# Laying a kernel's inputs out on the host: fewer, wider loads and no weight turns on TensorE

## The chip, the cores and the metric

The kernel runs on one core of a Trainium2 chip. The metric is the device time of one execution in microseconds, lower is better. A core has the engines TensorE (PE in the profile; PEld is its weight load), VectorE (DVE), ScalarE (ACT), GpSimd (POOL) and SyncE (SP). SP, ACT and POOL also issue DMAs; the suffix q in a row of the profile (SPq, ACTq) marks such an issue, and "landing" is the moment at which the whole transfer has arrived.

## The reference

Four layers in a row on x of 32 sequences x 32 tokens x 256 features (B, S, D). Each sequence has a role (1 or 2 of 3 possible) and a target code.

```python
# layers 0, 2 and 3: an adapter whose weights are picked by the role of the sequence
h = gelu(x @ W_down[role] + b_down[role])          # 256 -> 128, exact gelu
y = x + h @ W_up[role] + b_up[role]                # 128 -> 256
x = (y - mean(y)) * rsqrt(var(y) + 1e-5) * gamma[role] + beta[role]

# layer 1: attention over 32 tokens and two 4x-wide MLPs, the same weights for all
q, k, v = x @ Wq, x @ Wk, x @ Wv
a = softmax(q @ k.T / 16) @ v @ Wp + bp
cms = gelu(a @ cW1 + cb1) @ cW2 + cb2 + one_hot(code)
mod = gelu(concat(a, cms) @ mW1 + mb1) @ mW2 + mb2
x = clip(x + cms + mod, 0, 1)
```

## The kernel before

All tensors are float32; products whose precision matters are split into a high and a low part of a faster format (suffixes _h and _l in the names) and take three matmuls.

**Sorting by role.** The 1024 tokens are cut into 8 windows of 128 tokens (4 sequences). VectorE sorts the sequences by role at run time (`find_windows`, L1064 to L1109), so that six windows hold one role each and need one set of adapter weights, and two mixed windows (`MESSY`, 4 and 5) need two. One small TensorE product (`find_order`, L653) and one VectorE operation (L1114) turn the sort into token numbers `from_row_i`, by which POOL gathers the windows of x from HBM (L1485, tile `x_tok`). The roles of the windows go to SP, which reads them into registers and fetches each window's adapter weights (`fetch`, L559: one DMA for W_down, one for W_up).

**Set-up of layer 1.** Wq Wk^T and Wv Wp are multiplied once ("fold", L696), since the attention only needs the products. For this Wq, Wk and Wv are first turned on TensorE (`fold_transpose`, L684), copied out by ScalarE (L908), and then multiplied. The small vectors (biases, gamma, beta) are loaded as rows into `vec_rows`, 16 DMAs on three queues; one product picks the rows for each window (`chunk_vectors`, L670), and one turn makes `vecs`, one column for each vector of 128 (`vectors`, L646).

**Order.** Nothing is scheduled by a tool. The list in `plan` (L114) gives the steps in order, and each engine runs its part of each step in that order; `("fold", 0, 0)` is a step's name and its arguments. Engines meet on semaphores only. So a step of TensorE that waits holds up each step behind it in the list. The adapter chain of a window in layer 0 is `load` (turn x), `down`, gelu on ScalarE, `up`, statistics on VectorE (L1256), `center` (L1321), `turn`.

**DMA order.** SP issues its DMAs in the order of its block (L532), ACT those of L870 on, POOL five vector loads (L1481) and then the gathers.

Of the kernel before, what the change touches and what calls it, by code (L numbers as in the profile page):

```python
# [16 lines left out]
F32 = mybir.dt.float32  # L17
F32R = mybir.dt.float32r
I32 = mybir.dt.int32
# [5 lines left out]
P = 128  # L25
B, S, D = 32, 32, 256
N = B * S
R = 3
# [126 lines left out]
def build(nc, a, out):  # L155

    steps = plan()
    with ExitStack() as ctx:
# [20 lines left out]
        roles_i = place("roles_i", [P, B], I32)  # L179
# [23 lines left out]
        role_col_i = place("role_col_i", [B, 2], I32)  # L203
# [52 lines left out]
        wdA = [place(f"wdA{i}", [P, KD, P], F32) for i in range(WSLOTS)]  # L256
        wuA = [place(f"wuA{i}", [P, D], F32) for i in range(WSLOTS)]
        wdB = [place(f"wdB{i}", [P, KD, P], F32) for i in range(WSLOTS)]
        wuB = [place(f"wuB{i}", [P, D], F32) for i in range(WSLOTS)]
        last_at = {(layer, n): stage_at + 4 * D * (2 * len(LAST) * i + 2 * m) for i, layer in enumerate((2, 3))  # L260
                   for m, n in enumerate(range(SLOTTED, PASSES))}
        wd_last = {key: place(f"wd_last{key[0]}_{key[1]}", [P, KD, P], F32, offset) for key, offset in last_at.items()}
        wu_last = {key: place(f"wu_last{key[0]}_{key[1]}", [P, D], F32, offset + 4 * D) for key, offset in last_at.items()}
# [35 lines left out]
        vec_rows = place("vec_rows", [ROWS, P], F32, g_at)  # L299
# [7 lines left out]
        wT = {w: place(f"wT_{w}", [P, KD, D], F32) for w in "qkv"}  # L307
# [24 lines left out]
        codes_in = sem("codes_in")  # L332
        vectors_in = sem("vectors_in")
        mlp_vectors_in = sem("mlp_vectors_in")
# [3 lines left out]
        wdA_in = [sem(f"wdA_in{i}") for i in range(WSLOTS)]  # L338
        wuA_in = [sem(f"wuA_in{i}") for i in range(WSLOTS)]
        wdB_in = [sem(f"wdB_in{i}") for i in range(WSLOTS)]  # L340
        wuB_in = [sem(f"wuB_in{i}") for i in range(WSLOTS)]
        wd_last_in = {key: sem(f"wd_last_in{key[0]}_{key[1]}") for key in last_at}
        wu_last_in = {key: sem(f"wu_last_in{key[0]}_{key[1]}") for key in last_at}
        x_in = [sem(f"x_in{i}") for i in range(TSLOTS)]
        bu_in = sem("bu_in")
        bu_late_in = sem("bu_late_in")
# [13 lines left out]
        vectors_ps = sem("vectors_ps")  # L360
        vectors_ready = sem("vectors_ready")
        chunk_vecs_ready = sem("chunk_vecs_ready")
        wT_ps = sem("wT_ps")
        wT_ready = sem("wT_ready")
# [72 lines left out]
        def weights_of(layer, c):  # L437

            found = []
            for n in pass_of(layer, c):  # L440
                if (layer, n) in last_at:
                    found.append((wd_last[layer, n], wu_last[layer, n], wd_last_in[layer, n], wu_last_in[layer, n], 16))
                    continue
                kind, i = home(layer, n)
                down, up, down_in, up_in = (wdA, wuA, wdA_in, wuA_in) if kind == "A" else (wdB, wuB, wdB_in, wuB_in)
                s = i % WSLOTS
                found.append((down[s], up[s], down_in[s], up_in[s], 16 * (i // WSLOTS + 1)))
            return found
# [51 lines left out]
        def square(w):  # L500
            return tiled("qkvp".index(w) // 2)[:, KD * ("qkvp".index(w) % 2):KD * ("qkvp".index(w) % 2 + 1), :]
# [24 lines left out]
        down_w = {0: "L0_cond_W_down", 2: "L2_cond_W_down", 3: "L3_cond_W_down"}  # L526
        up_w = {0: "L0_cond_W_up", 2: "L2_cond_W_up", 3: "L3_cond_W_up"}

# [4 lines left out]
        def _(sp):  # L533
            sp.dma_start(roles_i[:, :], a["itok_B_1_2"].partition_broadcast(P)).then_inc(ids_in, 16)
            sp.dma_start(square("k"), a["L1_cond_Wk"].rearrange("(k p) n -> p k n", p=P)).then_inc(square_in["k"], 16)
            sp.dma_start(role_col_i[:, 1:2], a["itok_B_17_1546"].rearrange("(b o) -> b o", o=1)).then_inc(codes_in, 16)

            def piece(p):
                slot, _ = filling(p)
                src, view, _ = pieces[p]  # L540

                if p == 1:
                    sp.wait_ge(wT_ps, 2)
                elif p == 2:
                    sp.wait_ge(fold_ps, KD)
                elif p > 2:
                    sp.wait_ge(w_ready, p - STAGE + 1)
                sp.dma_start(view(slot), src).then_inc(stage_in[slot], 16)
# [10 lines left out]
            def fetch(layer, r, down, up, down_in, up_in):  # L559
                sp.dma_start(down[:, :, :],  # L560
                             a[down_w[layer]].rearrange("r (k p) n -> r p k n", p=P)[bass.ds(r, 1), :, :, :]
                             .rearrange("r p k n -> (r p) k n")).then_inc(down_in, 16)
                sp.dma_start(up[:, :],
                             a[up_w[layer]][bass.ds(r, 1), :, :].rearrange("r p n -> (r p) n")).then_inc(up_in, 16)

            def adapter_weights(layer, n):
# [3 lines left out]
                down, up, down_in, up_in = (wdA, wuA, wdA_in, wuA_in) if kind == "A" else (wdB, wuB, wdB_in, wuB_in)  # L570
# [6 lines left out]
                fetch(layer, role[column], down[slot], up[slot], down_in[slot], up_in[slot])  # L577
# [7 lines left out]
            for v, w in ((GAMMA2, "L2_cond_gamma"), (BETA2, "L2_cond_beta")):  # L585
                for m in range(KD):
                    sp.dma_start(vec_rows[R * (v + m):R * (v + m + 1), :],
                                 a[w][:, m * P:(m + 1) * P]).then_inc(vectors_in, 16)
# [19 lines left out]
            for layer, n in last_at:  # L608
                fetch(layer, role[passes_of(layer)[n][1]], wd_last[layer, n], wu_last[layer, n],
                      wd_last_in[layer, n], wu_last_in[layer, n])  # L610
# [13 lines left out]
        def _(pe):  # L624
# [21 lines left out]
            def vectors():  # L646
                pe.wait_ge(constants, 2)
                pe.wait_ge(vectors_in, (3 + 4 * KD) * 16)
                pe.wait_ge(mlp_vectors_in, 5 * 16)
                take(0, vectors_ready, 1)  # L650
                pe.transpose(bank[0][:, 0:ROWS], vec_rows[:, :], ident[0:ROWS, 0:ROWS]).then_inc(vectors_ps, 1)

            def find_order():  # L653
                pe.wait_ge(sorts_ready, 1)
                take(1, rows_in_ready, 1)
                pe.matmul(bank[1][:, 0:FULL], seat[:, :], rows_of[:, :], start=True, stop=True).then_inc(order_ps, 1)
# [9 lines left out]
            def chunk_vectors():  # L666
                pe.wait_ge(role_hot_ready, 1)
                pe.wait_ge(vectors_in, (3 + 4 * KD) * 16)
# [898 lines left out]
```

## Time and profile before

| | us |
|---|---|
| device time, median of 3 runs | 197.14 (196.89 to 197.19) |
| span of the profiled execution, first to last instruction | 196.6 |
| PE busy | 184.1 (94%) |
| DVE busy | 114.4 (58%) |
| ACT busy | 80.7 (41%) |
| POOL busy | 44.2 (22%) |

The profile holds no other time of the profiled execution than its span of 196.6 us; the median lies 0.54 us above it. Times in rows count from the first instruction. In rows of windows, counts of instructions stand in brackets, and the last three numbers are PE's granted clock, the DMA engines' busy share and GB/s. Busy PE is not PE at its peak: ends of matmuls are modelled. A float32 matmul is two PE instructions.

### The profile page before, as it was taken

Reading aid. Unit: us, or ns where it says so; the run is one execution under the profiler, and the core shown is the slowest. Engines: PE = TensorE matmul, PEld = TensorE weight load, DVE = VectorE, ACT = ScalarE, POOL = GpSimd, SP = SyncE. Lnnn points to the kernel's source line nnn. Section 1 sums busy time; section 2 is a strip of 40 time slices with the busy share of each in tenths; the row PEclk is TensorE's granted clock in tenths of the full one; section 3 lists DMA queues with packets and bytes.
Section 4 is the critical chain, followed back from the end, with each engine's and each line's share of the span. In section 5 each row is a group of like instructions: output and inputs, shape, how many; then the busy total and the mean of one; then the engine's idle time right before and its main releaser. Section 6 shows DMA issues by size and latency. Waiting matters only on the chain.

```text
span 196.6 us, 3109 instructions
## 1 busy us (share of the span) xinstructions
PE 184.1 (94%) x1031; PEld 157.7 (80%) x1031; DVE 114.4 (58%) x283; ACT 80.7 (41%) x164; POOL 44.2 (22%) x74
## 2 busy tenths in 40 slices
PE   7877999989999999999999999999999999999960
PEld 7755878878988888778888888888888989999840
DVE  2994998989648807983193522041442146569972
ACT  0733656544698405672045543003546242222420
POOL 8472848200000006000140000000110012234552
PEclk9999999999999999999999999999999999999995
DMA  3687389996300230330000060000100005433002
GB/s 110 224 243 242 97 259 294 245 312 187 107 3 8 100 107 0 107 110 0 0 0 3 0 196 18 0 0 3 55 0 0 3 0 141 125 85 107 28 27 80
DMA packets 18585, 17.82 MB, mean 91 GB/s; under 512 B 2049, under 2 KB 16970, under 8 KB 18570
## 3 DMA queue, kind: packets, MB, share of 16 engines
q1 hardware_dynamic: 16720, 14.60, 24.3%
q0 software_dynamic: 1024, 2.37, 4.5%
q10 hardware_dynamic: 826, 0.67, 1.1%
q8 instruction: 8, 0.13, 0.3%
q14 instruction: 7, 0.06, 0.1%
HBM read 16.58 MB, written 1.05 MB: 90 GB/s over the span
## 4 chain that ended last, share of the span: by engine, by line
PE 79%; DVE 8%; DMA 5%; issue 3%; ACT 2%; POOL 1%; ACTq 0%; DVEq 0%; POOLq 0%
PE bank L636 20%; PE bank L638 19%; PE bank L637 19%; PE bank L748 5%; PE bank L764 5%; DMA stage<-in_L_cond_Wq 2%; PE bank L741 2%; PE bank L815 2%; PE bank L804 2%; DMA x_tok<-in_x,from_row_i 2%; PE bank L774 1%; DVE yA L1321 1%; PE bank L743 1%; DMA out<-yB,from_row_i 1%; DVE cms_l L1423 1%
## 5 line engine op out<-in xcount | busy, mean ns | idle before, releaser
L1402 DVE TENSOR_TENSOR g_l<-g_full,g_h 128x512 fp32r<-128x512 f32 x32 | 21.8, 690 | 36.1 <-ACT g_h L1028 36.0
L1025 ACT ACTIVATE g_full<-bank,vecs 128x512 f32<-128x512 f32 x32 | 22.1, 691 | 43.5 <-PE bank L638 39.9
L1514 POOL TENSOR_TENSOR mvA<-mvA,power 128x1 f32<-128x1 f32 x16 | 9.4, 589 | 72.0 <-DVE mvA L1257 72.0
L1028 ACT ACTIVATE g_h<-bank,vecs 128x512 fp32r<-128x512 f32 x32 | 22.0, 686 | 0.0
L1541 POOL TENSOR_TENSOR x1T<-x1T,cms_full 128x512 f32<-128x512 f32 x4 | 6.0, 1497 | 57.4 <-DVE cms_full L1417 57.3
L636 PE MATMUL bank<-g_h,mw_h 128*128 128x256 f32 (+1 forms) x48 | 16.0, 334 | 0.0
L638 PE MATMUL bank<-g_h,mw_l 128*128 128x256 f32 (+1 forms) x48 | 15.3, 318 | 0.0
L637 PE MATMUL bank<-g_l,mw_h 128*128 128x256 f32 (+1 forms) x48 | 15.3, 318 | 0.0
L636 PE MATMUL bank<-ao_h,mw_h 128*128 128x512 f32 x32 | 13.1, 411 | 0.0
L636 PE MATMUL bank<-ao_h,cw_h 128*128 128x512 f32 x32 | 12.8, 400 | 0.1
L638 PE MATMUL bank<-ao_h,mw_l 128*128 128x512 f32 x32 | 12.5, 391 | 0.0
L637 PE MATMUL bank<-ao_l,mw_h 128*128 128x512 f32 x32 | 12.5, 390 | 0.0
L638 PE MATMUL bank<-cms_h,mw_l 128*128 128x512 f32 x32 | 12.5, 390 | 0.0
L638 PE MATMUL bank<-ao_h,cw_l 128*128 128x512 f32 x32 | 12.5, 390 | 0.0
L636 PE MATMUL bank<-cms_h,mw_h 128*128 128x512 f32 x32 | 12.5, 390 | 0.0
L637 PE MATMUL bank<-ao_l,cw_h 128*128 128x512 f32 x32 | 12.5, 390 | 0.0
L636 PE MATMUL bank<-g_h,cw_h 128*128 128x512 f32 x32 | 12.5, 389 | 0.0
L638 PE MATMUL bank<-g_h,cw_l 128*128 128x512 f32 x32 | 12.5, 389 | 0.0
L637 PE MATMUL bank<-cms_l,mw_h 128*128 128x512 f32 x32 | 12.5, 389 | 0.0
L637 PE MATMUL bank<-g_l,cw_h 128*128 128x512 f32 x32 | 12.4, 389 | 0.0
L1321 DVE TENSOR_SCALAR yA<-bank,mvA 128x256 f32<-128x256 f32 x16 | 8.6, 540 | 3.1 <-POOL mvA L1514 2.8
L1417 DVE TENSOR_TENSOR cms_full<-bank,target 128x512 f32<-128x512 f32 x4 | 2.8, 692 | 12.9 <-PE bank L638 12.9
(265 smaller groups left out, 442.8 us busy)
## 6 DMA issues: line engine op xcount, KB each, us to landing
stage<-in_L_cond_mW SPq DMA_DIRECT2D x6, 512.0 KB
stage<-in_L_cond_cW SPq DMA_DIRECT2D x4, 512.0 KB
wdA<-in_L_cond_W_down SPq DMA_DIRECT2D x14, 128.0 KB
wuA<-in_L_cond_W_up SPq DMA_DIRECT2D x14, 128.0 KB
wdB<-in_L_cond_W_down SPq DMA_DIRECT2D x12, 128.0 KB, 2.5
wuB<-in_L_cond_W_up SPq DMA_DIRECT2D x12, 128.0 KB, 2.8
wd_last<-in_L_cond_W_down SPq DMA_DIRECT2D x4, 128.0 KB, 2.3
wu_last<-in_L_cond_W_up SPq DMA_DIRECT2D x4, 128.0 KB, 2.5
```

Of the source, the lines that this page charges most:

```text
L636: pe.matmul(dst, w[0], x[0], start=first, stop=False)
L637: pe.matmul(dst, w[0], x[1], start=False, stop=False)
L638: return pe.matmul(dst, w[1], x[0], start=False, stop=last)
L741: pe.matmul(bank[b][:, m * P:(m + 1) * P], x[:, m, :], ident[:, :], start=(m == 0), stop=False, is_transpose=True, skip_group_check=True)
L748: mm = pe.matmul(bank[b][:, D + part * P:D + (part + 1) * P], wd[:, k, :], x[:, k, :], start=False, stop=(k == KD - 1), skip_group_check=True)
L764: mm = pe.matmul(dst, h[:, part, :], wu[:, :], start=False, stop=(part == len(turns) - 1), skip_group_check=True)
L1025: act.activation(g_full[n % 2][:, 0:width], bank[b][:, 0:width], ACT.Gelu, bias=bias)
L1028: act.activation(g[0][:, j, 0:width], bank[b][:, 0:width], ACT.Gelu, bias=bias).then_inc(g_high, 1)
L1321: dve.tensor_scalar(yA[k][:, :], bank[chain_bank(layer, c)][:, 0:D], mvA[:, k, 0:1], mvA[:, k, 2:3], ALU.subtract, ALU.mult).then_inc(norm ...
L1402: dve.tensor_tensor(g[1][:, j, 0:width], g_full[n % 2][:, 0:width], g[0][:, j, 0:width].bitcast(F32), ALU.subtract).then_inc(g_ready, 1)
L1514: pool.tensor_tensor(mv[:, k, 2:3], mv[:, k, 1:2], power[:, :], ALU.pow).then_inc(done, 1)
L1541: pool.tensor_tensor(half, half, cms_full[:, m, :], ALU.add).then_inc(sum_ready, 1)
```

## The change

The host, which before passed every input as it was, now passes repacked copies of the same numbers:

- `ids`: 128 rows of 34 numbers, the 32 roles and then this row's role and code. One DMA on SP in place of three on SP and ACT.
- `squares`: Wq, Wk and Wv already turned, Wp as it is, each as 128 rows of 2 KB. Four DMAs remain, first or second on their queues (before, 256 rows of 1 KB each, with Wv fourth and Wp fifth or later). The turns on TensorE and their copies on ScalarE go; the tiles `wT` are loaded directly, with one for p, and no longer share the `stage` slots.
- `vec_rows` and `vecs`: the rows that the picking products need in one DMA, and the turned vectors in another, both on ACT. The turn of `vec_rows` on TensorE and its copy on ScalarE go, with POOL's five loads.
- `b_up`: one DMA in place of three.
- `adapters`: a role's W_down and W_up side by side, 128 rows of 2 KB. `fetch` issues one DMA in place of two, with one semaphore. The 30 fetches of the program were 60 DMAs and are 30.

In `plan`, the two steps `fold_transpose` 0 and 1 and the three warm-up products go, and both steps of `fold` 0 stand ahead of `order`.

```diff
-        ("warm", 10), ("fold_transpose", 0), ("fold_transpose", 1), ("warm", 3), ("order",), ("pick_vecs",),
-        ("fold_transpose", 2), ("spread",), ("fold", 0, 0), ("first_hot",), ("fold", 0, 1), ("fold_low", 0),
-        ("fold", 1, 0), ("chunk_vecs",), ("vectors",), ("sort_rest",), ("load", 0, 0), ("fold", 1, 1),
+        ("warm", 10), ("fold", 0, 0), ("fold", 0, 1), ("order",), ("pick_vecs",), ("spread",), ("first_hot",),
+        ("fold_low", 0), ("fold", 1, 0), ("chunk_vecs",), ("sort_rest",), ("fold", 1, 1), ("load", 0, 0),
...
-            sp.dma_start(roles_i[:, :], a["itok_B_1_2"].partition_broadcast(P)).then_inc(ids_in, 16)
-            sp.dma_start(square("k"), a["L1_cond_Wk"].rearrange("(k p) n -> p k n", p=P)).then_inc(square_in["k"], 16)
-            sp.dma_start(role_col_i[:, 1:2], a["itok_B_17_1546"].rearrange("(b o) -> b o", o=1)).then_inc(codes_in, 16)
+            sp.dma_start(ids[:, :], a["ids"]).then_inc(ids_in, 16)
+            sp.dma_start(wT["k"][:, :, :], square_from("k")).then_inc(square_in["k"], 16)
+            sp.dma_start(wT["p"][:, :, :], square_from("p")).then_inc(square_in["p"], 16)
...
-            def fetch(layer, r, down, up, down_in, up_in):
-                sp.dma_start(down[:, :, :],
-                             a[down_w[layer]].rearrange("r (k p) n -> r p k n", p=P)[bass.ds(r, 1), :, :, :]
-                             .rearrange("r p k n -> (r p) k n")).then_inc(down_in, 16)
-                sp.dma_start(up[:, :],
-                             a[up_w[layer]][bass.ds(r, 1), :, :].rearrange("r p n -> (r p) n")).then_inc(up_in, 16)
+            def fetch(layer, r, w, w_in):
+                sp.dma_start(w[:, :], a["adapters"][(0, 2, 3).index(layer)][bass.ds(r, 1), :, :]
+                             .rearrange("r p n -> (r p) n")).then_inc(w_in, 16)
...
-            for m, w in enumerate(("L0_cond_b_up", "L2_cond_b_up", "L3_cond_b_up")):
-                sp.dma_start(bu_rows[0:2 * R, m, :],
-                             a[w].unsqueeze(0).to_broadcast([2, R, D])).then_inc(bu_late_in if m else bu_in, 16)
-            sp.dma_start(square("p"), a["L1_cond_Wp"].rearrange("(k p) n -> p k n", p=P)).then_inc(square_in["p"], 16)
+            sp.dma_start(bu_rows[0:2 * R, :, :], a["b_up"]).then_inc(bu_in, 16)
             piece(0)
...
-                    pe.wait_ge(wT_ready, 2 + n)
-                    if n:
-                        pe.wait_ge(square_in["p"], 16)
+                    pe.wait_ge(square_in[left], 16)
+                    pe.wait_ge(square_in[right], 16)
...
-            act.dma_start(role_col_i[:, 0:1], a["itok_B_1_2"].rearrange("(b o) -> b o", o=1)).then_inc(ids_in, 16)
-            act.dma_start(square("q"), a["L1_cond_Wq"].rearrange("(k p) n -> p k n", p=P)).then_inc(square_in["q"], 16)
...
+            for w in "qv":
+                act.dma_start(wT[w][:, :, :], square_from(w)).then_inc(square_in[w], 16)
+            act.dma_start(vec_rows[:, :], a["vec_rows"][0:PER_ROLE * R, :]).then_inc(vectors_in, 16)
+            act.dma_start(vecs[:, :], a["vecs"]).then_inc(vecs_in, 16)
...
-                dve.wait_ge(ids_in, 32)
+                dve.wait_ge(ids_in, 16)
```

TensorE's queue at the start of the program, before. `stage_121` holds Wq and Wk, `stage_122` Wv; the product with `rows_of` is the step `order`.

```order
L644 MATMUL bank<-warm 128x128 x9
L692 MATMUL bank<-ident,stage_121 128x128 [waits square_in_q,constants]
L692 MATMUL bank<-ident,stage_121 128x128 x3
L692 MATMUL bank<-ident,stage_121 128x128 [waits square_in_k,constants]
L692 MATMUL bank<-ident,stage_121 128x128 x3
L644 MATMUL bank<-warm 128x128 [waits warm_ready]
L644 MATMUL bank<-warm 128x128 x2
L656 MATMUL bank<-rows_of,seat 128x6 [waits sorts_ready]
L692 MATMUL bank<-ident,stage_122 128x128 [waits square_in_v,constants]
L692 MATMUL bank<-ident,stage_122 128x128 x3
L706 MATMUL bank<-wT_k,wT_q 128x256 [waits wT_ready,rows_in_ready]
L706 MATMUL bank<-wT_k,wT_q 128x256 x3
```

The same place in the changed kernel. `x_tok_189` and `x_tok_190` are the first two gathered windows of x.

```order
L613 MATMUL bank<-warm 128x128 x9
L654 MATMUL bank<-wT_k,wT_q 128x256 [waits square_in_k,square_in_q]
L654 MATMUL bank<-wT_k,wT_q 128x256 x3
L618 MATMUL bank<-rows_of,seat 128x6 [waits sorts_ready]
L654 MATMUL bank<-wT_p,wT_v 128x256 [waits square_in_p,square_in_v]
L654 MATMUL bank<-wT_p,wT_v 128x256
L632 MATMUL bank<-role_pick,vec_rows 128x66 [waits vectors_in,role_hot_ready]
L654 MATMUL bank<-wT_p,wT_v 128x256 x2
L669 MATMUL bank<-ident,x_tok_189 128x128 [waits x_in0,constants,rows_in_ready]
L669 MATMUL bank<-ident,x_tok_189 128x128
L669 MATMUL bank<-ident,x_tok_190 128x128 [waits x_in1,xA_ready]
L669 MATMUL bank<-ident,x_tok_190 128x128
```

The product of `order` now has four matmuls of 256 columns ahead of it, where it had eight turns and three warm-ups, and between the two loads of x no fold matmul is left: all eight stand ahead of the first load.

SP's queue from the moment at which the windows' roles are known, before:

```order
L554 TENSOR_LOAD chunk_role_i [waits chunks_ready]
L560 ISA
L560 DMA wdA_124<-in_L_cond_W_down 128x2x128
L563 DMA wuA_128<-in_L_cond_W_up 128x256
L560 ISA
L560 DMA wdA_125<-in_L_cond_W_down 128x2x128
L563 DMA wuA_129<-in_L_cond_W_up 128x256
```

And changed:

```order
L534 TENSOR_LOAD chunk_role_i [waits chunks_ready]
L540 ISA
L540 DMA wA_123<-in_adapters 128x512
L540 ISA
L540 DMA wA_124<-in_adapters 128x512
```

Each pair of DMAs of a window has become one DMA of the same bytes.

## Rows read from the trace of the kernel before

**Rows 1.** Windows: stretch, length, busy us of PE, PEld, DVE, ACT, POOL, clock, DMA.
```profile
14.00:17.00 3.00, 2.02 (x16) 1.81 (x17) 1.73 (x10) 0.53 (x2) 1.75 (x2) 1.00 1.01 326
...
20.00:25.00 5.00, 4.82 (x35) 3.96 (x34) 4.83 (x18) 3.46 (x11) 3.59 (x5) 1.00 0.47 121
...
80.00:180.00 100.00, 99.85 (x534) 85.54 (x533) 45.03 (x86) 35.64 (x66) 10.99 (x14) 1.00 0.15 44
```
**Rows 2.** Timeline, 0 to 20 us: start, us, engine, line, what, count, idle before.
```profile
0.73 0.42 SPq L534 DMA_DIRECT2D roles_i<-in_itok_B  x1
...
1.06 4.21 PE L644 MATMUL bank<-warm 128*128 128x128 f32 x20 [1.06 <-DVE warm L1065]
...
1.20 0.47 ACTq L874 DMA_DIRECT2D stage<-in_L_cond_Wq  x1
1.21 0.42 SPq L535 DMA_DIRECT2D stage<-in_L_cond_Wk  x1
...
4.48 0.18 DVE L1076 TENSOR_SCALAR roles<-roles_i 128x32 f32<-128x32 int32 x1 [1.88 <-DMA role_col_i<-in_itok_B]
...
6.93 0.83 PE L644 MATMUL bank<-warm 128*128 128x128 f32 x6
...
7.13 0.28 DVE L1103 TENSOR_SCALAR rows_of<-window_of,is_full,row_col 32x6 f32<-32x6 f32 x1
...
7.70 0.38 PE L656 MATMUL bank<-rows_of,seat 32*128 32x6 f32 x2
...
8.62 1.06 POOL L1485 DMA_INDIRECT x_tok<-in_x,from_row_i  x1 [2.61 <-DVE from_row_i L1114]
...
14.29 0.01 SPq L560 DMA_DIRECT2D wdB<-in_L_cond_W_down  x1
...
15.71 0.01 SPq L563 DMA_DIRECT2D wuB<-in_L_cond_W_up  x1
15.75 0.37 ACT L923 COPY xA<-bank 128x256 f32<-128x256 f32 x1 [1.59 <-PE bank L719]
...
17.31 0.62 ACT L940 ACTIVATE hA<-bank,chunk_vecs 128x128 f32<-128x128 f32 x2 [1.19 <-PE bank L748]
...
18.47 0.43 DVE L1256 BATCH_NORM_STATS2 statsA<-bank 128x6 f32<-128x256 f32 x1 [2.68 <-PE bank L764]
```
**Rows 3.** DMA issues: what, queue, count, KB each, median us to landing.
```profile
wdB<-in_L_cond_W_down SPq DMA_DIRECT2D x12, 128.0 KB, 2.5
...
stage<-in_L_cond_Wq ACTq DMA_DIRECT2D x1, 256.0 KB, 4.7
stage<-in_L_cond_Wk SPq DMA_DIRECT2D x1, 256.0 KB, 4.4
...
x_tok<-in_x,from_row_i POOLq DMA_INDIRECT x8, 3.9
...
roles_i<-in_itok_B SPq DMA_DIRECT2D x1, 16.0 KB, 2.9
role_col_i<-in_itok_B ACTq DMA_DIRECT2D x1, 0.1 KB, 3.7
```
**Rows 4.** The chain of waits: start, us, what.
```profile
8.62 3.50 DMA x_tok<-in_x,from_row_i
...
12.67 0.87 PE bank L706 x4
```
**Rows 5.** Timeline near the end of the program.
```profile
179.29 0.37 SPq L560 DMA_DIRECT2D wdB<-in_L_cond_W_down  x1
...
183.39 1.06 PE L748 MATMUL bank<-zB,wdB 128*128 128x128 f32 x8
```
**Rows 6.** Windows again, around the last matmuls.
```profile
189.00:191.00 2.00, 1.30 (x8) 0.70 (x6) 1.38 (x5) 0.37 (x1) 1.36 (x3) 1.00 0.18 66
191.00:192.40 1.40, 0.00 (x0) 0.00 (x0) 1.15 (x4) 0.00 (x0) 1.17 (x1) 1.00 0.00 0
192.40:194.00 1.60, 0.00 (x0) 0.00 (x0) 0.82 (x2) 0.00 (x0) 0.58 (x1) 0.50 0.57 164
```

More of the change, by code:

```diff
@@ L178, in build @@
         scratch = at[0]
-        roles_i = place("roles_i", [P, B], I32)
+        ids = place("ids", [P, B + 2], I32)
+        roles_i = ids[:, 0:B]
+        role_col_i = ids[0:B, B:B + 2]
         roles = place("roles", [P, B], F32)
@@ L306, in build @@
         y_T = place("y_T", [P, KD, HALF], F32, at[0])
-        wT = {w: place(f"wT_{w}", [P, KD, D], F32) for w in "qkv"}
+        wT = {w: place(f"wT_{w}", [P, KD, D], F32) for w in "qkvp"}
         wqk = [place(f"wqk_{x}", [P, KD, D], F32R) for x in "hl"]
@@ L569, in adapter_weights @@
                 slot = i % WSLOTS
-                down, up, down_in, up_in = (wdA, wuA, wdA_in, wuA_in) if kind == "A" else (wdB, wuB, wdB_in, wuB_in)
+                w, w_in = (wA, wA_in) if kind == "A" else (wB, wB_in)
                 if i >= WSLOTS:
@@ L644, in keep_warm @@
                     pe.matmul(bank[7][:, 0:P], warm[:, :], warm[:, :], start=True, stop=True)
[L646 to L651, printed above, removed]
             def find_order():
                 pe.wait_ge(sorts_ready, 1)
-                take(1, rows_in_ready, 1)
-                pe.matmul(bank[1][:, 0:FULL], seat[:, :], rows_of[:, :], start=True, stop=True).then_inc(order_ps, 1)
+                take(2, rows_in_ready, 1)
+                pe.matmul(bank[2][:, 0:FULL], seat[:, :], rows_of[:, :], start=True, stop=True).then_inc(order_ps, 1)
             def rest():
@@ L761, in up @@
                 turns = weights_of(layer, c)
-                for part, (_, wu, _, w_in, filled) in enumerate(turns):
-                    pe.wait_ge(w_in, filled)
-                    mm = pe.matmul(dst, h[:, part, :], wu[:, :], start=False, stop=(part == len(turns) - 1),
+                for part, (w, _, _) in enumerate(turns):
+                    mm = pe.matmul(dst, h[:, part, :], w[:, D:2 * D], start=False, stop=(part == len(turns) - 1),
                                    skip_group_check=True)
@@ L859, in outer @@
                             mm.then_inc(outer_ps, 1)
-            do = {"warm": keep_warm, "vectors": vectors, "order": find_order, "rest": rest, "chunk_vecs": chunk_vectors, "seq_vecs": seq_vectors,
-                  "codes": codes_sorted, "fold_transpose": fold_transpose, "fold": fold,
+            do = {"warm": keep_warm, "order": find_order, "rest": rest, "chunk_vecs": chunk_vectors, "seq_vecs": seq_vectors,
+                  "codes": codes_sorted, "fold": fold,
                   "load": load, "down": down, "up": up, "turn": turn, "values": values, "project": project, "scores": scores, "mix": mix,
@@ L1557 @@
     arrays, aps = {}, {}
-    for name, value in inputs.items():
-        if name == "_lenS":
-            continue
+    laid = {name: np.asarray(value) for name, value in inputs.items()}
+    by_role = [(f"L{n}_cond_b_down", 1) for n in (0, 2, 3)]
+    for n in (0, 2):
+        by_role += [(f"L{n}_cond_gamma", KD), (f"L{n}_cond_beta", KD)]
+    vec_rows = [laid[name][:, m * P:(m + 1) * P] for name, tiles in by_role for m in range(tiles)]
+    vec_rows += [laid[f"L1_cond_{name}"].reshape(-1, P) for name in ("bp", "cb1", "cb2", "mb1", "mb2")]
+    vec_rows = np.concatenate(vec_rows)
+    ids = np.stack([laid["itok_B_1_2"], laid["itok_B_17_1546"]], axis=1)
+    packed = {
+        "x": laid["x"],
+        "ids": np.concatenate([np.broadcast_to(laid["itok_B_1_2"], (P, B)), np.tile(ids, (P // B, 1))], axis=1),
+        "vec_rows": vec_rows,
+        "vecs": vec_rows.T,
+        "b_up": np.stack([np.tile(laid[f"L{n}_cond_b_up"], (2, 1)) for n in (0, 2, 3)], axis=1),
+        "squares": np.stack([w.reshape(KD, P, D).transpose(1, 0, 2) for w in (
+            laid["L1_cond_Wq"].T, laid["L1_cond_Wk"].T, laid["L1_cond_Wv"].T, laid["L1_cond_Wp"])]),
+        "adapters": np.stack([np.concatenate([
+            laid[f"L{n}_cond_W_down"].reshape(R, KD, P, P).transpose(0, 2, 1, 3).reshape(R, P, KD * P),
+            laid[f"L{n}_cond_W_up"]], axis=2) for n in (0, 2, 3)]),
+    }
+    packed.update((name, laid[name]) for name in (
+        "L1_cond_cW1", "L1_cond_cW2", "L1_cond_mW1", "L1_cond_mW2", "L3_cond_ln_w", "L3_cond_ln_b"))
+    for name, value in packed.items():
         v = np.ascontiguousarray(value)
```

111 lines of the change are left out of this document (31 added, 80 removed).

## The prediction

> **What bounds the kernel now.** I read three things in this order. First the windows: from 80 to 180 us PE is busy 99.85 of 100 us [rows 1], so that stretch has no hole that an earlier load could fill, and its length is set by matmuls that the change does not touch. Then the chain of waits and the timeline of the first 20 us [rows 2], since the chain leaves PE there: it goes from the squares' DMAs to PE, from PE to VectorE's token numbers, to the first gather of x, and from there through the first windows of layer 0. VectorE's first statistics start at 18.47 after 2.68 us of idling for PE; from then on VectorE is the full engine (4.83 of 5 us from 20 to 25 [rows 1]) until the dense stretch of PE begins. So the front is one chain up to 18.47: what moves that start moves the rest of the program with it, one for one, and what does not move it is worth nothing. Last the tail, because the adapter fetches change there too.
>
> The sum is made against the span of 196.6 us, and 0.54 us is added to get to the median of 197.14.
>
> **The ids.** The sort waits for two DMAs. `roles_i`, issued at 0.73, lands 2.9 us later [rows 2, 3], at 3.63. The column of 32 single numbers lands 3.7 us after its own issue on ACT, and it is this one that VectorE waits for: `roles` starts at 4.48, with the column named as the releaser [rows 2]. The one DMA `ids` has `roles_i`'s place, its 128 rows and nearly its bytes, so I take its 2.9: the sort starts near 3.67, 0.8 us earlier. Bounds: 2.9 (gain 0.8) and the column's 3.7 (gain 0). `rows_of`, the sort's last result for the gathers, ends at 7.41 = 7.13 + 0.28 [rows 2]; it would end at 6.6.
>
> **PE ahead of `order`.** Today the product starts at 7.70, 0.3 us after `rows_of`, because the three warm-ups (six instructions, 6.93 to 7.76) stand ahead of it [rows 2]. In the changed kernel fold 0 stands there. The ten first warm-ups run from 1.06 to 5.27 [rows 2] and stay. Two fold matmuls (four instructions) take 0.87 us of the chain [rows 4], so fold's four take 1.74. It needs q and k, which now land at 1.20 + 4.7 = 5.90 and 1.21 + 4.4 = 5.61 [rows 2, 3]. q moves to the head of ACT's queue, 0.46 us earlier, with half the packets; k keeps its place. I take both at 5.3, hence fold from 5.3 to 7.05 and `order` at 7.1, against 7.70: gain 0.6. What the sort has won beyond that (ready at 6.6) is lost behind fold. Bounds: with q and k in before 5.27 the gain is 0.65; with them where they are now (5.90), fold ends at 7.65 and it is 0; a later landing is rival 3.
>
> **The gather and layer 0.** The first gather follows `order` by 0.92 us (8.62 against 7.70 [rows 2]) and its x lands after 3.50, at 12.12 [rows 4]. So it is issued at 8.0, and x lands at 11.5. POOL's five vector loads are worth nothing: POOL idles 2.61 us for VectorE's token numbers behind them [rows 2], and still will. The windows' weights move earlier as well, since the sort's roles do, and SP then issues one DMA for a window where it issued two; this is beside the path. Two things could pull at the gain. More adapter bytes are queued by the time the gathers' packets run: the median gather takes 3.9 [rows 3], and if the first goes from its 3.5 to 3.9, 0.4 is lost. And `fold` 1 no longer stands between the two loads of x: 0.87 us of PE [rows 4] that lay in the wait for the second gather, worth 0. I keep 0.6.
>
> **The rest at nothing.** The turns and copies of squares and vectors on PE and ACT: the cover is the gather's flight of 3.5 us, and the only turns on the path are those ahead of `order`, already counted. The loads of `b_up` and of the vectors' rows: no wait in the first 20 us is put down to one of them. The fetches for layers 2 and 3 land long before use. The closest is the last: issued at 179.29, its W_down lands after 2.5 us and is used in the second half of the eight instructions from 183.39 [rows 3, 5], about 183.9. The joined DMA carries 128 KB more, 0.4 us at the 326 GB/s of rows 1; even with 0.9 it is in by 182.7, 1.2 us early. If that cover went, the end would be later by the rest.
>
> **Sum.** 196.6 - 0.6 = 196.0 us of span, and 196.5 us of time.
>
> **The clock rule.** Rows first: the twenty first warm-up instructions take 4.21 us, 0.21 each, the six later ones 0.83, 0.14 each [rows 2]: the early ones run at the lower of the two levels (1.2 GHz), the later at 2.4. At the end the granted clock falls from 1.00 to 0.50 at 192.4, behind 1.30 us of busy PE from 189 to 191 and 1.4 us of none [rows 6]. The Trainium skill (TensorE: Matmul & The Clock Gate, Part 1: The HAM clock gate) says that the low level is the default and that activity alone lifts it. That speaks against the change, which takes filler out of the wait for x; by it the saving can turn into a loss (rival 2). By the three stretches of rows 1, where the clock is 1.00 even at two thirds of busy time, nothing would be lost.
>
> **Rival 1: SP's and ACT's stalls go too.** At 14.29 and 15.71 SP's DMA issues take 0.01 us, where they otherwise take 0.42, and come 1.4 us apart; in the same stretch ACT copies the second window only at 15.75, after 1.59 us of idling for a turn on PE, and the gelu starts at 17.31 after 1.19 [rows 2], while the DMA engines are full (1.01 of the time [rows 1]). If both come of SP's queue being full, half the DMAs end it, and the window chain gains at most the two waits, 2.8 us, and at least nothing. For: SP and ACT go on in the same moment (15.71, 15.75). Against: nothing names the cause, and the bytes stay the same. I take 1.2 more than the forecast: 195.3.
>
> **Rival 2: the clock falls while PE waits for x (slower).** Place: behind the last fold matmul. From 5.3 the folds (3.5 us), `order` (0.4 [rows 2]) and the chunk vectors' product (about as much) end near 9.6, at most 10. x lands at 11.5, and the second window near 13 (8.0, 1.06 for the first issue, 3.9). PE has some 3 us with the two turns of the first window in them and nothing else. The tail shows a fall behind 3.4 us that held 1.3 [rows 6]. Against it: the wait for the first x today, behind folds and small products, costs no clock. Price: PE is busy 2.02 us from 14 to 17 [rows 1], and at half the clock that is 2.0 us more at most, and 0 where it hides behind the gathers; I take 1.5. It decides from a loss of 0.6 on. Time: 197.1 - 0.6 + 1.5 = 198.0.
>
> **Rival 3: fold holds up `order`.** All four squares are now asked for at once, with cW1 behind them. Today's landings of q and k have v beside them; one more square of 256 KB ahead of them is 0.8 us at 326 GB/s. Then k lands at 6.4, fold ends at 8.15, and the gather is 0.45 late: 197.6. If q and k come first on their two queues, as they are issued, they land between 5.3 and 5.9, and at the late end nothing changes: 197.1. The Trainium skill (DMA: Bandwidth & Descriptors, Issuing engines are not separate DMA queues) says that DMAs of different issuers interleave on the same engines. By it v competes with k and p with v, which leads to this rival; k's 4.4 [rows 3] agrees, as far as it goes, since q has the same bytes and 4.7.
>
> **Chances.** Forecast 47%, with its own range 196.2 to 196.9. Rival 1 20%. Rival 2 14%. Rival 3 19%, of which 13 end near no change and 6 slower. A measurement of this kernel can tell about 0.2% (0.4 us) from no change. Faster than 196.75: 40 of the forecast's 47 and rival 1, 60%. Within 0.2%: 7 and 13, 20%. Slower than 197.53: 14 and 6, 20%. The range runs from 195.2 to 197.9: it leaves out the lower part of rival 1 and the upper of rival 2, under 2 in 10.
>
> **What would show each step.** `roles` starting near 3.7 and `rows_of` ending near 6.6: the ids. Fold's first matmul at 5.3 and `order` right behind its last, near 7.1: the hand-over; an `order` product later than 7.7 is rival 3. The gather at 8.0, the first statistics near 17.9, with VectorE idle ahead of them as now: the shift. Statistics near 16.7, with SP's issues evenly spaced: rival 1. A granted clock under 1.00 between 10 and 20 us: rival 2. If the statistics come 0.6 earlier and the end does not, the front is not one chain, and "one for one" is the wrong step; the place to look is then between 20 us and the dense stretch. The forecast is wrong altogether if the time moves while the first statistics stay.

## The result and the profile after

The changed kernel takes 199.98 us (median of 4 executions, 198.38 to 200.43) against 197.16 of the kernel before: 1.0111 times as long, 95% interval 1.0060 to 1.0161. Twelve more executions gave 199.99 and 1.0115 (1.0076 to 1.0153). The forecast was 196.5, with a range up to 197.9. The profiled execution has a span of 198.4 and a time of 200.24. In all later runs time and span differ by 1.8, of the kernel before too (109 executions beside the experiments: median span 195.3, median time 197.09). A ratio leaves out executions far above the fastest of its kernel; where the clock falls in most executions but not in all, these are ordinary ones, and there the median tells more.

The chain of waits of the changed kernel, 0 to 20 us, its pieces in order of time (start us, us, what):

```profile
1.05 4.63 PE bank L613 x20
5.68 2.13 PE bank L654 x8
7.82 0.33 PE bank L618 x2
...
8.69 1.15 POOL x_tok L1419
...
10.14 5.63 DMA x_tok<-in_x,from_row_i
...
15.91 0.66 PE bank L669 x2
...
17.21 0.85 PE bank L699 x4
```

The chain goes over the second gather, which takes 5.63 us. In the rows of before it went over the first (3.50 [rows 4]) and then over PE's work; in a second profile of that kernel (below) it goes over the second gather too, which takes 3.92 us there. The timeline of the same stretch (start us, us, engine, line, what; idle before it, ended by what):

```profile
3.45 0.18 DVE L1014 TENSOR_SCALAR roles<-ids 128x32 f32<-128x32 int32 x1 [0.86 <-DMA ids<-in_ids]
...
5.48 2.34 PE L654 MATMUL bank<-wT_k,wT_q 128*128 128x256 f32 x8
...
6.11 0.28 DVE L1041 TENSOR_SCALAR rows_of<-window_of,is_full,row_col 32x6 f32<-32x6 f32 x1
...
7.75 0.38 PE L618 MATMUL bank<-rows_of,seat 32*128 32x6 f32 x2
...
8.14 1.92 SPq L540 DMA_DIRECT2D wA<-in_adapters  x4
...
8.69 1.15 POOL L1419 DMA_INDIRECT x_tok<-in_x,from_row_i  x1 [5.42 <-DVE from_row_i L1052]
...
13.15 0.62 PE L669 MATMUL bank<-ident,x_tok 128*128 128x128 f32 x2 [2.21 <-DMA x_tok<-in_x,from_row_i]
...
15.91 0.66 PE L669 MATMUL bank<-ident,x_tok 128*128 128x128 f32 x2 [2.14 <-DMA x_tok<-in_x,from_row_i]
...
20.54 0.43 DVE L1193 BATCH_NORM_STATS2 statsA<-bank 128x6 f32<-128x256 f32 x1 [4.86 <-PE bank L714]
```

Against [rows 2]: the sort starts 1.03 us earlier and ends 1.02 earlier, but `order` is at 7.75 (7.70 before), since fold 0 is ahead of it until 7.82. The statistics come at 20.54, 2.07 later than in the row of before, and 3.8 later than in its second profile (16.71). The windows of the stretch (length, busy us of PE, PEld, DVE, ACT, POOL, then the granted clock, DMA share, GB/s) show what happens to PE while it waits:

```profile
10.00:12.00 2.00, 0.94 (x4) 0.49 (x3) 1.86 (x9) 0.72 (x2) 1.55 (x2) 1.00 0.93 319
12.00:14.00 2.00, 0.62 (x2) 0.25 (x2) 1.86 (x14) 0.19 (x1) 1.39 (x3) 0.80 1.05 398
14.00:16.00 2.00, 0.09 (x1) 0.12 (x2) 1.64 (x8) 0.18 (x1) 1.70 (x2) 0.50 0.91 305
16.00:18.00 2.00, 2.00 (x10) 2.00 (x11) 0.00 (x0) 0.37 (x1) 0.17 (x1) 0.50 0.37 105
18.00:20.00 2.00, 2.00 (x11) 2.00 (x10) 0.00 (x0) 0.74 (x2) 0.00 (x0) 0.50 0.00 0
20.00:25.00 5.00, 5.00 (x35) 4.25 (x34) 4.14 (x18) 2.42 (x7) 2.95 (x4) 1.00 0.09 24
```

With 0.94, 0.62 and 0.09 us of work in three times 2 us, the clock falls to 0.50 (1.2 GHz) and stays there until 20 us, over the first windows' products. Four of them on L699 take 0.85 us of the chain, where four take 0.44 from 27.84 on, at full clock. The DMA issues answer to [rows 3] (KB each, median us to landing; x before 3.9, q 4.7, k 4.4):

```profile
wA<-in_adapters SPq DMA_DIRECT2D x14, 256.0 KB, 4.0
...
wT_q<-in_squares ACTq DMA_DIRECT2D x1, 256.0 KB, 3.0
...
wT_k<-in_squares SPq DMA_DIRECT2D x1, 256.0 KB, 3.6
...
x_tok<-in_x,from_row_i POOLq DMA_INDIRECT x8, 4.4
```

### The profile page after: what moved, and what is told of

It is laid out like the page before. It is cut to its first block, busy times and chain, and to the rows that moved or that the text cites. A ratio compares the mean times of both kernels' runs of the same rounds, so it can differ in the third digit from the quotient of the medians.

```text
span 198.4 us, 2982 instructions
## 1 busy us (share of the span) xinstructions
PE 184.8 (93%) x1012; PEld 158.2 (80%) x1012; DVE 114.4 (58%) x283; ACT 79.4 (40%) x160; POOL 41.5 (21%) x69
## 4 chain that ended last, share of the span: by engine, by line
PE 81%; DVE 8%; DMA 4%; issue 2%; POOL 2%; ACT 1%; DVEq 0%; POOLq 0%; ACTq 0%
PE bank L605 20%; PE bank L607 19%; PE bank L606 19%; PE bank L699 6%; PE bank L714 5%; DMA x_tok<-in_x,from_row_i 3%; PE bank L613 2%; PE bank L692 2%; PE bank L765 2%; PE bank L754 2%; PE bank L724 1%; DVE yA L1258 1%; PE bank L694 1%; PE bank L654 1%; DMA out<-yB,from_row_i 1%
## 5 line engine op out<-in xcount | busy, mean ns | idle before, releaser
L1193 DVE BATCH_NORM_STATS2 statsA<-bank 128x6 f32<-128x256 f32 x16 | 6.8, 422 | 6.8 <-PE bank L714 6.5
```

The source lines that it names most:

```text
L1193: link(dve.bn_stats(st[:, k, 0:6], y))
```

## The experiments

The theories: G, the adapter fetches, which now leave SP at one of 256 KB per 0.52 us (8.14 to 10.24 for four), slow the gathers of x; C, the clock's fall in the wait is what costs; F, fold 0 ahead of `order` eats what the ids gain. "Gathers" below are the times from POOL's issue of the first and of the second gather to their turn on PE. Each ratio is to the kernel before on the same chip.

**Fillers (C).** The diff is in `plan`:

```diff
-("fold", 1, 1), ("load", 0, 0), ("load", 0, 1),
+("fold", 1, 1), ("warm", 8), ("load", 0, 0), ("warm", 6), ("load", 0, 1),
```

> The changed kernel with filler products on PE in its two waits for x: eight (16 instructions) behind the last fold matmul and six (12) between the turns of the first and of the second window. If the clock's fall is what costs (theory C), the granted clock stays 1.00 from 7 to 20 us, the products of the first windows take 0.45 again where they took 0.85, the first statistics come at 19.2 or before instead of 20.54, and the time falls by 1.3 or more, to 198.6. If the late landing of x is what costs (theory G: the second window's x at 15.8), the clock stays up too but PE still turns the second window at 15.9, and at most half of it comes back: statistics near 19.9, time near 199.4.

Measured: 197.86 us, ratio 1.0048 (1.0026 to 1.0071), clock 0.992 to 0.997 in all ten executions. Gathers 4.60 and 5.40 us, statistics at 18.50. The windows in which the clock had fallen, and two lines of the timeline:

```profile
12.00:14.00 2.00, 1.44 (x13) 1.28 (x13) 1.86 (x14) 0.00 (x0) 1.60 (x2) 1.00 1.02 367
14.00:16.00 2.00, 1.49 (x14) 1.31 (x12) 1.87 (x10) 0.37 (x1) 1.49 (x2) 1.00 0.83 308
```

```profile
15.81 0.41 PE L669 MATMUL bank<-ident,x_tok 128*128 128x128 f32 x2 [0.51 <-DMA x_tok<-in_x,from_row_i]
...
18.50 0.43 DVE L1193 BATCH_NORM_STATS2 statsA<-bank 128x6 f32<-128x256 f32 x1 [2.56 <-PE bank L714]
```

The second turn is where it was (15.81 against 15.91), and the statistics come 2.0 us earlier. So 2.1 us of the loss hang on the clock, more than the 1.3 of theory C, and the gathers are about as slow as without the fillers.

**Order first (F).** Three filler products are added ahead of it.

```diff
-("warm", 10), ("fold", 0, 0), ("fold", 0, 1), ("order",),
+("warm", 13), ("order",), ("fold", 0, 0), ("fold", 0, 1),
```

> The changed kernel with the order product ahead of fold 0 and three more filler products ahead of it. If fold 0 in front of it (at the low clock level until 6.4 us) is what ate the ids' gain (theory F), order runs at 6.7 instead of 7.75, the first gather goes at 7.6 instead of 8.69, and all that follows comes 1.0 earlier: first statistics at 19.5, time 199.0. If the landing of x is set by what the DMA engines carry (theory G), the adapters' fetches of SP are not earlier in this kernel (chunk_role_i has the same time), the gathers go ahead of them, and x comes earlier by more than 1.0: statistics near 18.7, time near 198.2. If neither, 200.

Measured: 198.10 us, 1.0037 (0.9996 to 1.0077). Its timeline:

```profile
6.34 0.38 PE L618 MATMUL bank<-rows_of,seat 32*128 32x6 f32 x2 [0.79 <-DVE rows_of L1041]
...
7.31 1.14 POOL L1419 DMA_INDIRECT x_tok<-in_x,from_row_i  x1 [4.05 <-DVE from_row_i L1052]
...
14.41 0.66 PE L669 MATMUL bank<-ident,x_tok 128*128 128x128 f32 x2 [2.60 <-DMA x_tok<-in_x,from_row_i]
```

The product now waits for `rows_of` and not for PE's queue, and the gathers start 1.4 us earlier. The second still takes 5.65 us, and the clock still falls in most executions: 194.5 us of span in the one at clock 0.995, 197.1 in one at 0.974. F holds: the edit alone repairs 1.9 us. Not all of it need be `order` itself, since the clock is at 0.981 or more in eight of ten executions, where it is in two of sixteen of the changed kernel.

**Fetches held (G).** In SP's loop over layer 0's fetches:

```diff
+                if n == 2:
+                    sp.wait_ge(x_in[1], 16)
                 adapter_weights(0, n)
```

> The changed kernel in which SP holds back the adapter fetches from the third window's on until the second window's x is in. Theory G: the six fetches of 256 KB that are issued from 8.1 to 11.1 us slow the gathers; with two of them only, x lands 3.5 to 4.0 us after its issue (first 12.4, second 14.1 instead of 15.8), the statistics come near 18.6 and the time is near 198.0 if nothing later waits for the held fetches. Theory C or F alone: the gathers land as before (13.1 and 15.8), time 200.

Measured: 195.22 us, 0.9903 (0.9869 to 0.9937): 4.8 us less than the changed kernel, and faster than the kernel before. I had expected 198.0. Its timeline:

```profile
12.32 0.41 PE L671 MATMUL bank<-ident,x_tok 128*128 128x128 f32 x2 [1.12 <-DMA x_tok<-in_x,from_row_i]
...
13.32 0.41 PE L671 MATMUL bank<-ident,x_tok 128*128 128x128 f32 x2 [0.59 <-DMA x_tok<-in_x,from_row_i]
...
16.17 0.43 DVE L1195 BATCH_NORM_STATS2 statsA<-bank 128x6 f32<-128x256 f32 x1 [0.25 <-PE bank L716]
```

Gathers of 3.37 and 2.92 us, though `order` is at 8.01 here. With x in time PE has work, and the clock held in four of five executions. The second turn comes 2.6 us earlier than in the changed kernel, which with the 2.1 us of the clock is about the 4.8. The hold thus mends two of the three causes.

**Rate or size of the pieces?** Four kernels change only how SP sends the adapters of layer 0. Two DMAs of 1 KB pieces for a role:

```diff
-                sp.dma_start(w[:, :], a["adapters"][(0, 2, 3).index(layer)][bass.ds(r, 1), :, :]
-                             .rearrange("r p n -> (r p) n")).then_inc(w_in, 16)
+                for lo in (0, D):
+                    sp.dma_start(w[:, lo:lo + D], a["adapters"][(0, 2, 3).index(layer)][bass.ds(r, 1), :, lo:lo + D]
+                                 .rearrange("r p n -> (r p) n")).then_inc(w_in, 16)
```

> The changed kernel with each role's adapters fetched by two DMAs of 1 KB pieces instead of one of 2 KB: same bytes, same layout in memory, twice the DMAs. If the joining of the fetches (quicker issue, 2 KB pieces) is what slows the gathers, the second window's x lands 3.9 to 4.4 after its issue (14.2) instead of 5.6, the first statistics come near 19, time near 198.5. If the squares' and the other loads' new times do it, or the clock alone, it stays at 200.

Two DMAs of 64 partitions, pieces of 2 KB (`lo in (0, P // 2)`, `w[lo:lo + P // 2, :]`):

> The changed kernel with each role's adapters fetched by two DMAs of 64 partitions with pieces of 2 KB, against the two DMAs of 128 partitions with pieces of 1 KB of an earlier run (x landed 3.3 and 4.0 us after issue, time 198.3): the same bytes at the same rate of issue, only the pieces differ. If the size of the pieces is what slows the gathers (G-size), they take 4.4 and over 5 us and the time is 199.7. If it is the rate at which bytes are queued (G-rate), they take 3.3 and 4.0 and the time is 198.3.

One or two DMAs of 8 bytes behind each fetch:

```diff
                 adapter_weights(0, n)
+                sp.dma_start(pace[0:1, 2 * n:2 * n + 2], a["ids"][0:1, 0:2]).then_inc(pace_in, 16)
```

> The changed kernel with its 2 KB pieces and one DMA for a role's adapters, but a DMA of 8 bytes behind each of the ten fetches of layer 0 on SP, which holds SP for about 0.4 us: a fetch every 0.9 us instead of every 0.5. If it is the rate at which SP queues bytes (256 KB in 0.5 us) that slows the gathers (theory G-rate), x lands as with two DMAs to a role: first 3.3 and second 3.9 after issue; time like that kernel's, 198.3, or less where the clock holds. If it is the size of the pieces (G-size), the gathers stay at 4.4 and 5.7 us and the time at 200.

> The changed kernel with joined 2 KB pieces in one DMA, and two DMAs of 8 bytes behind each of layer 0's fetches, so one fetch every 1.25 us (205 GB/s) where one small DMA gave 0.87 us (301 GB/s; x landed 3.75 and 4.85 us after issue, 199.7). Theory G-rate: at this rate the engines have room and x lands 3.4 and 3.9 us after issue; time 198.3 or less, since nothing but the clock and fold 0 is then left. If it is the joining itself that slows the gathers and not the rate, 4.4 or more for the second and 199.7 again.

| fetches | us per 256 KB | GB/s asked for | gathers, us | time, us | ratio |
|---|---|---|---|---|---|
| changed kernel | 0.52 | 500 | 4.46, 5.77 | 199.98 | 1.0111 |
| one small DMA between | 0.88 | 298 | 3.78, 4.90 | 199.70 | 1.0126 (1.0066 to 1.0186) |
| kernel before, second profile | 1.08 | 243 | 3.17, 4.05 | 197.13 | |
| two of 1 KB pieces | 1.04 | 252 | 3.27, 3.99 | 198.33 | 1.0015 (0.9970 to 1.0059) |
| two small DMAs between | 1.18 | 222 | 3.52, 3.83 | 198.44 | 0.9965 (0.9903 to 1.0028) |
| two of 64 partitions | 1.33 | 196 | 3.63, 3.90 | 198.62 | 1.0068 (1.0026 to 1.0109) |

The second gather goes with the rate and not with the pieces: 2 KB pieces at 196 and 222 GB/s let it land as quickly as 1 KB pieces do. Nor is it, at the full rate, the number of fetches already out: with order first the second gather was issued 0.7 us behind the first fetch (8.76 and 8.04) and took 5.65, with 1 KB pieces 1.5 us behind it (9.44 and 7.92) and took 3.99. My expectation that 0.88 us would be slow enough was wrong. From the two paced kernels, the timelines (second gather's issue, second turn; first the one of 0.88, then the one of 1.18):

```profile
10.13 0.97 POOL L1423 DMA_INDIRECT x_tok<-in_x,from_row_i  x1 [0.30 <-issue]
...
15.03 0.66 PE L673 MATMUL bank<-ident,x_tok 128*128 128x128 f32 x2 [2.15 <-DMA x_tok<-in_x,from_row_i]
```

```profile
9.56 0.97 POOL L1424 DMA_INDIRECT x_tok<-in_x,from_row_i  x1 [0.30 <-issue]
...
13.39 0.41 PE L674 MATMUL bank<-ident,x_tok 128*128 128x128 f32 x2 [1.35 <-DMA x_tok<-in_x,from_row_i]
```

The three slower rates do not bring the kernel back to 195, because the clock falls in most of their executions: with two small DMAs between, one at clock 0.997 took 195.19 us, nine at 0.973 to 0.982 took 197.21 to 199.54.

**The kernel before, again.**

> The kernel before, unchanged, for a second profile. The other executions of it have spans of 194.8 to 196.1, the profiled one that the prediction was worked out from 196.6. If that one had a rare wait in it (SP's and ACT's stall near 15.7 us), this profile shows the second window's copy on ACT near 14.5 instead of 15.75, the first statistics near 17.2 instead of 18.47, and a span of 195.2. If not, the statistics come at 18.4 again and the difference lies elsewhere.

Measured: 197.13 us, profiled span 194.8. Its timeline:

```profile
9.94 1.02 POOL L1485 DMA_INDIRECT x_tok<-in_x,from_row_i  x1 [0.30 <-issue]
...
13.99 0.41 PE L719 MATMUL bank<-ident,x_tok 128*128 128x128 f32 x2 [0.98 <-DMA x_tok<-in_x,from_row_i]
14.10 0.42 SPq L563 DMA_DIRECT2D wuB<-in_L_cond_W_up  x1
...
14.44 0.37 ACT L923 COPY xA<-bank 128x256 f32<-128x256 f32 x1 [0.81 <-PE bank L719]
...
16.71 0.43 DVE L1256 BATCH_NORM_STATS2 statsA<-bank 128x6 f32<-128x256 f32 x1 [0.95 <-PE bank L764]
```

The stall of SP and ACT in [rows 2] is not in it. So the rows of before come from an execution with a wait that not every execution of the kernel has. How rare it is is not shown: two executions have a profile, and 16 of the 109 others took over 198.2 us.

**Parts alone, on the kernel before.** The ids in one DMA:

> The kernel before with the ids alone in one DMA. rows_of is ready at 6.4 instead of 7.4, but the order product stands behind two turns of squares, that wait for q until 6.0, and six filler instructions: theory F (PE's queue ahead of order decides, not the ids) says order at 7.3 to 7.65 and a time within 0.4 of before, 196.7 to 197.0. If the ids alone were worth what they come earlier, order would be at 6.7 and the time 196.1.

Measured: 196.16 us, 0.9959 (0.9931 to 0.9988); `order` at 6.66. I had expected next to nothing. `rows_of` was ready at 6.07, and PE's turns and six fillers were through at about 6.7, so the queue held `order` back by 0.6 and not by more. The joined adapters (one DMA of 2 KB pieces in `fetch`):

> The kernel before with the adapters alone joined: one DMA of 2 KB pieces for a role in place of two of 1 KB, on all fetches, nothing else changed. Theory G says that this part alone makes the kernel slower: x lands 4.4 and over 5 us after issue instead of 3.2 and 4.0, the second window's turn is at 15.3 instead of 14.0, and the time is 198.4, up to 200 where the clock falls in the wait. If joining is harmless and the squares' earlier loads or the shorter PE work are the cause, it stays at 197.

Measured: 198.84 us, 1.0083 (1.0046 to 1.0120). Its second gather:

```profile
10.41 1.02 POOL L1489 DMA_INDIRECT x_tok<-in_x,from_row_i  x1 [0.30 <-issue]
...
16.22 0.41 PE L723 MATMUL bank<-ident,x_tok 128*128 128x128 f32 x2 [1.90 <-DMA x_tok<-in_x,from_row_i]
```

5.81 us: this part alone, in an otherwise unchanged kernel, makes the whole delay of the gather. It costs 1.4 us of time (197.41 for the kernel before on this chip) without a fall of the clock: the granted clock is 1.00 in every window of this profile from 0 to 22 us. The hold without the change:

> The kernel before with the adapter fetches held from the third window's on until the second window's x is in; nothing of the change. In the second profile of the kernel before x lands 3.2 and 4.0 us after issue. Theory G: the second falls to 3.0, its turn goes from 13.99 to 12.96 and the time from 197.0 to 196.1, so the changed kernel with the same hold (195.2) keeps 0.9 us that are the change's own (earlier ids, fewer issues). If the hold alone were the whole gain, this kernel would take 195.2 too.

Measured: 196.83 us, 0.9991 (0.9974 to 1.0008): nothing that counts, where I had expected 196.1. At 243 GB/s there is little to hold back. Ids, joined adapters and hold together:

> The kernel before with the ids in one DMA, the joined adapters and the hold of the fetches until the second window's x is in; squares, vectors and b_up as before. It tells what the rest of the change (squares turned on the host, fewer vector loads) is worth: if nothing, this kernel equals the changed one with order first and the hold, 194.7. If the rest is worth its PE work ahead of the first turns, it stands at 195.5 to 196.0.

Measured: 195.60 us, 0.9898 (0.9844 to 0.9951), within the 195.5 to 196.0 that was expected if the rest has a worth of its own.

**Together.** Order first and hold; the same with four and two fillers; order first, with each of the third to the sixth fetch held for its own gather (`if 2 <= n < len(EARLY): sp.wait_ge(x_in[n - 1], 16)`):

> The changed kernel with both repairs: the order product ahead of fold 0, and the adapter fetches from the third window's on held until the second window's x is in. If the two add up, the gathers go at 7.3 and x lands at 10.6 and 11.6, but PE is then in the folds until 10.7; the first statistics come at 14.7 to 15.2 instead of 16.2 and the time is 193.8. If the fetches' hold is then the limit (a later window's weights come late), 195.2, as with the hold alone.

> As the kernel before in this list, with four filler products behind the last fold matmul and two between the first two turns. If the clock falls there in some executions (theory C), they end that: time 193.8 with a narrower spread and clock 0.997. If it doesn't fall, the six fillers (0.28 us each) delay the turns by up to 1.0 us and it is slower than without: 194.5.

> The changed kernel with the order product ahead of fold 0, and each adapter fetch from the third to the sixth held until the x of the window before it is in (so one fetch of 256 KB per 1.27 us, the distance of the gathers, about 206 GB/s), in place of one hold of all of them that is followed by a burst. If the burst behind the single hold costs something (there the fourth window's turn of x waited at 17.57), this is the fastest kernel: 194.0 or less, against 194.7. If the single hold already takes all there is, 194.7.

Measured: 194.69 us, 0.9879 (0.9819 to 0.9940), statistics at 14.95, clock 0.991 to 0.994; 194.91 with fillers; 194.92 with the finer hold. The three can't be told apart, and none reached the best that was expected of it (193.8, 193.8 and 194.0). Against the 195.60 of the kernel with ids, joined adapters and hold alone, 0.9 us are left for the turned squares, the vectors and the place of `order`, though the two intervals overlap. Two repairs without the hold:

> The changed kernel with two DMAs of 1 KB pieces to a role (x lands 3.3 and 4.0 us after issue, time 198.3 with a clock of 0.974 in most executions) and with the filler products of the first run in both waits for x. Theory: the gathers are already quick there and the low clock is what is left, so with the clock at 1.00 the time is 195.6, near the one execution of that kernel that kept its clock (195.60 at 0.996). If the clock is a symptom and costs nothing, 198.3.

Measured: 196.75 us, 0.9959 (0.9918 to 1.0000), clock 0.989 to 0.997. The clock is thus worth 1.6 us here. The other 1.2 I had expected are not there. In the profiled execution `order` is late, at 7.80 (7.05 without the fillers), the first turn, at 12.61, comes right behind the sixteen filler instructions and waits for no DMA, and the second gather takes 4.40, not 3.99.

> The changed kernel with the order product ahead of fold 0 and the filler products in both waits for x, and with the quick fetches as they are (one for 0.5 us). Clock and order are repaired, the gathers' slowing is left: x lands 4.0 and 5.5 us after issue (7.3 and 8.8), the second turn is at 14.3, statistics at 16.9, time 196.2, against 194.7 with the hold: 1.5 us for the gathers alone. If order first and fillers are already all, 194.7.

Measured: 197.12 us, 1.0001 (0.9973 to 1.0029), 0.9 more than expected. The third gather, issued at 10.01, held PE:

```profile
16.61 0.41 PE L669 MATMUL bank<-ident,x_tok 128*128 128x128 f32 x2 [0.53 <-DMA x_tok<-in_x,from_row_i]
```

That is 6.60 us after its issue. Against the same kernel with the hold (194.91) it is 2.2 us slower. Not all of this is the gathers': that kernel has eight products of filler fewer, and here the first two turns (12.54 and 14.09) wait for no DMA but stand behind the fillers. Last, the changed kernel again:

> The changed kernel, unchanged, beside the kernel before on the same chip, for a ratio over more runs and a second profile. All theories: near 199.5, ratio 1.011 to 1.014; executions at a granted clock of 0.97 about 2 us above those at 0.99.

Measured: 199.99 us, 1.0115 (1.0076 to 1.0153); gathers 4.61 and 5.43 us, clock under 1.00 from 12 to 20 us, statistics at 19.79. The executions at 0.972 and 0.973 took 199.51 to 200.72, those at 0.979 to 0.981 took 197.62 to 200.43, the one at 0.988 took 198.64. So the clock of an execution does not settle its time.

## Why the prediction was wrong

The step that failed is "The gather and layer 0". It put the joined fetches "beside the path" and kept a gain of 0.6 us. In its place the runs showed the second gather 1.7 us slower, a fall of the clock in the longer wait that costs 2.1 us, and 1.4 us of loss from the joined fetches alone, on the kernel before. "PE ahead of `order`" failed too, by 0.65 us.

- **The ids: right.** `roles` at 3.45 and `rows_of` done at 6.39 (forecast 3.67 and 6.6). On the kernel before, the part alone was worth 0.8 us by its ratio and 1.2 by the medians on that chip.
- **PE ahead of `order`: wrong.** The forecast has fold 0 from 5.3 to 7.05 and `order` at 7.1, with a loss only from a late landing. The squares landed early (q at 0.74 + 3.0, k at 1.21 + 3.6), so rival 3's cause is refuted, though its sign, an `order` later than 7.7, came. But the 1.74 us came from a row at the full clock. The ten first fillers took 4.63 us (4.21 in [rows 2]), 0.23 an instruction, where the added ones behind the folds take 0.125 (twelve in 1.50 us), and the fold behind them 2.34, where it takes 1.99 behind `order`. That these instructions ran at the lower clock is read from their length alone: the granted clock reads 1.00 in all windows from 0 to 10 us. In nine profiles with this order of steps `order` was at 7.05 to 8.02. `rows_of` waits 1.4 us for PE in the profile after; order first gives it back.
- **The gather: wrong, and the largest error.** The step says "this is beside the path" of the fetches, and prices a slower gather at 0.4 for the first one. The bytes are the same, but the second DMA of each window had also been a brake: 128 KB per 0.5 us is less than the 398 GB/s of the engines' fullest window above, 256 KB per 0.5 us is more. From issue to turn the first gather lost 0.8 us against the rows of before (4.46 and 3.64) and 1.3 against the second profile (3.17), the second gather 1.7 (5.77 and 4.05), and the chain goes over the second. The step looked only at the first, and took the median of [rows 3] as its price. Rival 2 has the second, at 13; it was in at 15.8.
- **The clock: the mechanism was rival 2, too low in chance and price.** Its place (behind the last fold matmul) and its sign came true. It had 14%, and the wait was taken for 3 us. The later and slower gathers made it 5.0 us, from the end of the folds at 10.9 to 15.9, with the same two turns. The price of 1.5 us measured 2.1 (fillers on the changed kernel) and 1.6 (with quick gathers). The two causes feed each other, so their shares depend on the order of repair; but the 1.4 us of the joined fetches alone came without a fall of the clock in the profile.
- **Rival 1: no effect.** Its stall is in one of the two profiles of before, and the change brought no gain of that kind.
- **One for one: right.** Span minus the start of the statistics is 177.8 to 178.1 in 19 of the 20 profiles read here (177.9 after, 178.1 before), for starts from 14.95 to 20.54. The exception is the kernel before with the hold, 178.6; its PE waits for gathers at 21.49 and 23.20, 0.5 and 0.6 us. That VectorE is the full engine from 20 us on is not shown: PE has 4.82 of 5 us beside its 4.83 [rows 1], and after the change PE has 5.00 and VectorE 4.14.
- **The base.** The 0.54 us join the span of one execution to the median of others: with the 1.8 us of all other executions, a span of 196.6 makes a time of about 198.4 (an estimate). This did not move the forecast, which in effect takes 0.6 off the median. It did hide that the statistics of before start at 16.7 in its second profile, not at 18.5.

## What to carry to other kernels

Fewer, larger DMAs also change how fast a queue is filled. Ask for each joined load how many GB/s its issuer now asks for, against what the engines carried in their fullest stretch, and what small, urgent transfer is issued just behind. Where the answer is over it, let the loads that are not urgent wait for the urgent one. To stay under it is no proof of safety: the gather took 4.9 us beside fetches at 298 GB/s, where the fullest window carried 398. Here one wait turned a kernel 1.1% slower than before into one 1.0% faster, and with `order` first 1.2%. And an idle stretch of TensorE that looks free may not be: add what the next products cost at the low clock.

## What the runs showed of the hardware

- The second gather of 128 rows of 1 KB was turned 2.9 to 4.1 us after its issue in the five kernels with a hold where PE waited for it, with only two fetches of 256 KB out before it. It took 3.5 to 4.4 beside fetches at 196 to 252 GB/s (six profiles), 4.9 at 298 (one profile) and 5.4 to 5.8 at about 500 (five profiles). The Trainium skill (DMA: Bandwidth & Descriptors, Queues, rings and completion order) says that each engine goes round the queues that have work, a packet at a time. That a gather lands later the more of the time SP's queue has work is in line with it; no run here shows the turns themselves. The size of the pieces made no difference here.
- The clock fell in PE's wait for x in some executions of a kernel and not in others, with equal code: ten executions with two DMAs of 1 KB pieces gave clocks from 0.973 to 0.996 and times from 195.60 to 199.97. The Trainium skill (TensorE: Matmul & The Clock Gate, Part 1: The HAM clock gate) says that the point of the rise varies from run to run; the first twenty filler instructions, which take 3.92 to 4.64 us in the nine profiles above, agree. A single profile of such a kernel is one draw.
- What is not settled: from which rate on the second gather is slowed (298 GB/s gave 4.90, 252 gave 3.99 and, with the gather issued 0.75 us later, 4.40); and how the loss divides between clock and gathers, which depends on the order in which they are repaired.
